# A decoder layer on one core: the side steps of a batch at other tiles of the written order

## The reference, cut to what matters

```
x = x + self_attention(layernorm(x))           # one head of 128, scores 256 x 256 per batch
x = x + cross_attention(layernorm(x), context) # 16 heads of 64, scores 256 x 1601 per head and batch
x = x + chosen_tokens_block(layernorm(x))      # router weight per token; the 31 best of 256 per batch
                                               # go through attention (16 heads of 8) and a GELU layer
```

## Time and profile before

| | |
|---|---|
| median of three executions | 2321.48 us |
| profiled execution | 2324.74 us |
| its span, first to last instruction | 2323.5 us |
| TensorE busy | 2154.8 us, 93% |
| GpSimd busy | 1916.2 us, 82% |
| ScalarE busy | 1844.7 us, 79% |
| VectorE busy | 1799.3 us, 77% |
| mean granted TensorE clock | 0.990 of full speed |
| first tile's exponential | 47.3 us |
| last tile's exponential | 2276.4 us |

### The profile page before, as it was taken

The page is one execution under the profiler, slowest core; times in us unless marked ns, Lnnn a source line. Parts: engine busy times, 40 slices in busy tenths (PEclk is TensorE's granted clock), DMA queues, the critical chain, the costliest instruction groups (busy, mean ns, idle before and its releaser), DMA issues.

```text
span 2323.5 us, 58064 instructions
## 1 busy us (share of the span) xinstructions
PE 2154.8 (93%) x22151; PEld 1566.6 (67%) x22151; DVE 1799.3 (77%) x3728; ACT 1844.7 (79%) x3125; POOL 1916.2 (82%) x1112
## 2 busy tenths in 40 slices
PE   8899999999998999999999899999999999999998
PEld 5567666766766666676767666677676666667665
DVE  5777878787787878877787888877878778786765
ACT  4788887888886888887978778788787788778872
POOL 1789888988987888888888788888898888888992
PEclk8999999999999999999999999999999999999999
DMA  2010000000000000000000000000000000000000
GB/s 67 28 49 13 1 2 12 2 13 1 12 2 1 12 2 13 2 11 12 2 12 2 1 12 2 12 2 21 2 2 12 2 12 2 2 2 11 2 1 10
DMA packets 17221, 22.15 MB, mean 10 GB/s; under 512 B 5601, under 2 KB 14834, under 8 KB 16946
## 3 DMA queue, kind: packets, MB, share of 16 engines
q1 hardware_dynamic: 15842, 18.24, 2.8%
q10 hardware_dynamic: 1104, 0.20, 0.1%
HBM read 16.20 MB, written 2.10 MB: 8 GB/s over the span
## 4 chain that ended last, share of the span: by engine, by line
PE 32%; DVE 7%; ACT 7%; issue 6%; POOL 2%; DVEq 0%; ACTq 0%; POOLq 0%
PE PS L525 6%; PE PS L563 5%; PE PS L526 5%; PE PS L542 5%; PE PS L544 4%; PE PS L589 3%; DVE EH L1026 2%; ACT PF L844 2%; POOL EL L1496 2%; DVE over L1049 2%; ACT over L866 1%; ACT EH L851 1%; PE PS L573 1%; ACT AH L880 1%; PE PS L599 1%
## 5 line engine op out<-in xcount | busy, mean ns | idle before, releaser
L1496 POOL TENSOR_TENSOR EL<-PF,EH 124x1024 f16<-124x1024 f32 x828 | 1761.2, 2149 | 255.1 <-ACT PF L844 75.0
L844 ACT ACTIVATE PF<-PS 124x512 f32<-124x512 f32 x1664 | 978.8, 600 | 264.1 <-PE PS L526 249.6
L542 PE MATMUL PS<-Ch,EH 123*128 123x97 f16 (+1 forms) x6656 | 768.0, 207 | 65.6 <-POOL EL L1496 50.9
L542 PEld LDWEIGHTS PS<-Ch,EH 123*128 123x128 f16 (+1 forms) x6656 | 608.8, 98 | 239.2 <-issue 123.7
L544 PE MATMUL PS<-Cl,EL 123*128 123x97 f16 (+1 forms) x6656 | 764.7, 207 | 0.0
L1026 DVE TENSOR_SCALAR_CACHE_REDUCE EH<-PF 124x1024 f16<-124x1024 f32 x621 | 746.7, 1208 | 20.1 <-ACT PF L844 18.7
L544 PEld LDWEIGHTS PS<-Cl,EL 123*128 123x128 f16 (+1 forms) x6656 | 598.6, 98 | 167.4 <-issue 3.0
L1049 DVE CUSTOM_DVE_ANT_1 over<-over,PS 128x806 f32<-128x806 f32 x512 | 506.4, 989 | 223.8 <-PE PS L563 132.9
L525 PE MATMUL PS<-AH,ChT 97*124 97x512 f16 x1664 | 648.9, 390 | 26.3 <-ACT PF L844 24.8
L526 PE MATMUL PS<-AL,ClT 96*124 96x512 f16 x1664 | 635.5, 382 | 0.0
L866 ACT ACTIVATE over<-PS 128x806 f32<-128x806 f32 x512 | 431.8, 843 | 46.9 <-PE PS L563 23.9
(11 more groups left out here) (234 smaller groups left out, 1834.7 us busy)
## 6 DMA issues: line engine op xcount, KB each, us to landing
Cf<-in_ctx SPq DMA_DIRECT2D x16, 546.0 KB
X<-in_x SPq DMA_DIRECT2D x16, 128.0 KB, 2.3
out_x<-X SPq DMA_DIRECT2D x16, 128.0 KB, 1.7
msk<-in_attention_mask SPq DMA_DIRECT2D x4, 256.0 KB, 4.3
AH<-mh SPq DMA_DIRECT2D x63, 2.0 KB
Cf<-in_ctx SPq DMA_DIRECT2D x16, 53.6 KB
xWqT<-in_xWqT SPq DMA_DIRECT2D x2, 256.0 KB, 6.3
xWo<-in_xWo SPq DMA_DIRECT2D x2, 256.0 KB, 3.8
```

Of the source, the lines that this page charges most:

```text
L542: pe.matmul(PS[:, 6, u0:u0 + DC + 1], EH[0:kr, r, qs], Ch[j][0:kr, t, :], start=(t == 0 and q == 0), stop=False, skip_group_check=True)
L844: act.activation(PF[:, n % PRING, :], PS[0:KP, 4 + n % 2, :], ACT.Exp).then_inc(sg("ex"), 1)
L1496: pool.tensor_tensor(EL[:, r - 1:r + 1, :], PF[:, f - 1:f + 1, :], EH[:, r - 1:r + 1, :], ALU.subtract).then_inc(sg("lo_pool"), 1)
```

## The change

Only places in the written order change. No step is added or removed, and no instruction is another.

- Self attention: first four steps from tiles 4, 6, 8, 10 to 5, 7, 10, 12; `sa_turn` from 30 to 29; its layer norm from 36 to 37.
- Context split: `ctx_hi` from tiles 9 and 11 to 8 and 7 (second half first).
- Choice: `sel_row` from 34 to 35, the first `sel_count` from 35 to 33, the second from 37 to 38, `sel_rank` from 44 to 48.
- Context transposes: the first from 58 to 55, `keys` from 63 to 64.
- Scale: `ctx_max` from 60 to 58, `sigma` from 71 to 68, `ctx_scale` from 75 to 73; `ln0` from 99 to 101.
- Sums' turns: both transposes of a quarter two tiles earlier, `proj` as before. In a batch they stand at 19 and 21, 45 and 47, 71 and 73, 97 and 99.
- Chosen tokens: six places per batch (82, 84, 86, 88, 90, 97) become five (82, 83, 84, 87, 94). The gather stands at 82 of a group's first batch in both. Rotation (`c_rope`): from tile 89 to 95 of the first batch. Values, turned queries and keys (`c_val`, `c_tqk`, `c_keys`): from 90, 97 and 98 of the first batch to 82, 83 and 84 of the second. The last steps (`c_down`, `c_scat`) go from the third batch to the fourth.

```
-SA_PLACES = (4, 6, 8, 10, 30, 32, 56)
-SEL_PLACE = 34
-TURN_PLACES = (58, 60, 62, 64)
-SIGMA_PLACE = 71
-CHOSEN_PLACES = (82, 84, 86, 88, 90, 97)
+SA_PLACES = (5, 7, 10, 12, 29, 32, 56)
+SEL_PLACE = 35
+TURN_PLACES = (55, 60, 62, 64)
+SIGMA_PLACE = 68
+CHOSEN_PLACES = (82, 83, 84, 87, 94)
...
-                 (SEL_PLACE + 1, ("sel_count", b - 1, 0)), (SEL_PLACE + 3, ("sel_count", b - 1, 1)),
-                 (SEL_PLACE + 10, ("sel_rank", b - 1))]
+                 (SEL_PLACE - 2, ("sel_count", b - 1, 0)), (SEL_PLACE + 3, ("sel_count", b - 1, 1)),
+                 (SEL_PLACE + 13, ("sel_rank", b - 1))]
...
-        todo += [(SIGMA_PLACE - 11, ("ctx_max", b + 2)), (SIGMA_PLACE, ("sigma", b + 2)),
-                 (SIGMA_PLACE + 4, ("ctx_scale", b + 2))]
-        todo += [(95, ("ln_stats0", b + 2)), (99, ("ln0", b + 2))]
+        todo += [(SIGMA_PLACE - 10, ("ctx_max", b + 2)), (SIGMA_PLACE, ("sigma", b + 2)),
+                 (SIGMA_PLACE + 5, ("ctx_scale", b + 2))]
+        todo += [(95, ("ln_stats0", b + 2)), (101, ("ln0", b + 2))]
...
-        todo += [(split + 1, ("ctx_hi", n, 0)), (split + 3, ("ctx_hi", n, 1))]
+        todo += [(split, ("ctx_hi", n, 0)), (split - 1, ("ctx_hi", n, 1))]
...
-        todo += list(zip(TURN_PLACES, transposes_of(n))) + [(TURN_PLACES[1] + 3, ("keys", n))]
+        todo += list(zip(TURN_PLACES, transposes_of(n))) + [(TURN_PLACES[1] + 4, ("keys", n))]
...
-        todo += list(zip((*q[:6], q[5] + 4, q[5] + 10, q[6]), self_attention(n)[2:]))
+        todo += list(zip((*q[:6], q[5] + 5, q[5] + 10, q[6]), self_attention(n)[2:]))
...
-        for late, step in ((1, ("turn_u", 0)), (3, ("turn_u", 1)), (5, ("proj",))):
+        for late, step in ((-1, ("turn_u", 0)), (1, ("turn_u", 1)), (5, ("proj",))):
```

## The result

The changed kernel takes 2263.07 us (median of 4 runs, 2257.95 to 2267.62) beside 2322.68 us for the kernel before on the same chip (2320.55 to 2326.45): ratio 0.9741, 95% interval 0.9713 to 0.9769. That is 60 us less where 43 were forecast; 2263.07 lies 15 us under the forecast, inside its range. Between the two profiled executions it is 57.1 us: span 2266.4 against 2323.5. (The profiled execution of the changed kernel is the longest of its four, 2267.62 us.)

What follows compares the result with a forecast made beforehand. TensorE, busy 93% of the span, was taken as the bound, so only its idle time could change. 3.0 us per batch times 14, plus 0.5 each for batches 0 and 15, gave -43: 2278.5 us, range 2262 to 2292.

Steps and rivals of the forecast that it cites:

- Start, 0.9: Self attention and context split, tiles 4 to 14: earlier exponentials on ScalarE win 0.9 us per batch, bounds 0 and 1.21.
- Choice, 1.7: Selection and sums' turns, tiles 26 to 50: 0.63 plus 1.30 us of waits won, taken as 1.7 per batch.
- gone or under 0.3 us: Sign: TensorE's waits at tiles 13, 14, 34, 40, 50 and 77 vanish or fall under 0.3 us each.
- Context turns, sigma, 0.3: Tiles 55 to 77: 0.7 and 0.66 us won, 0.45 and 0.6 lost, sum 0.3 us per batch.
- the rest, 0.1: Layer norm at tile 101 and the turns at 97 and 99: 0.1 us won per batch.
- Chosen tokens, 0: Chosen tokens' steps at their new places: 0 for a group of four batches, bounds -7 and +21 us.
- Some 4 us again: Rotation at tile 95 holds the fold of tile 96, which TensorE needs at 99: a wait of some 4 us.
- Rival 3: Slower: steps at 82, 83, 84 share one bank; 7.35 us per group batch, 66 in all, 2344.5 us; chance 0.13.
- Batch 15, -0.5: Last batch, which has no self attention: 0.5 us won.
- Rival 2: Key products at tile 84 stretched beside a fed GpSimd: 6 us lost per group, 18 in all, 2296.5 us; chance 0.12.
- Rival 1: GpSimd's run is the real bound: only 1.0 us per batch won, 14 in all, 2307 us; chance 0.15.
- Rival 4: Nearly all idle time goes, 4.5 us per batch, and four low clocks (12 us): 2246.5 us; chance 0.07.

Runs made afterwards that it cites:

- the start alone: Kernel before with only self attention's first four steps at tiles 5, 7, 10, 12 and the context split's first halves at 8 and 7: 2298.11 us, ratio 0.9897.
- the spread places: Changed kernel with chosen steps that use the bank two tiles apart or more, on own places in each of a group's four batches: 2237.37 us, ratio 0.9625.
- the chosen places alone: Kernel before with only the chosen tokens' new places (82, 83, 84, 87, 94): 2333.81 us, ratio 1.0046.
- the choice without the rank: Kernel before with row at 35, counts at 33 and 38, self attention's turn at 29, layer norm at 37, rank still at 44: 2315.89 us, ratio 0.9963.
- the context steps alone: Kernel before with context transposes from 55, keys 64, maxima 58, sigma 68, scaling 73, layer norm 101, sums' turns unmoved: 2324.5 us, ratio 1.0005.
- the turns alone: Kernel before with only both transposes of the sums two tiles earlier: 2377.49 us, ratio 1.0221.
- the context steps with the turns: Kernel before with context transposes, keys, maxima, sigma, scaling and layer norm at their changed places, plus the sums' transposes two tiles earlier: 2379.74 us, ratio 1.0236.
- the rank alone: Kernel before with only the rank block moved from tile 44 to 48: 2296.74 us, ratio 0.9892.

## Why the prediction was right, point by point

- **Start, 0.9.** Right in its mechanism, and small: 1.3 alone. I held back 0.3 for a chain on VectorE (low split, maxima) that turned out to leave ScalarE only 0.32 us. TensorE's two waits were 1.21. Batch 0, put at 0.5, won 4.1, and 3.6 of that comes with the start alone.
- **Choice, 1.7.** Right. The parts measured are 0.5 (choice) and 1.5 (rank), 2.0 against the 1.93 summed; GpSimd's run did take back most of the 0.79 and 1.55. The rank brought 0.2 more than its wait. The early count was covered by 1.0 us, the figure of the prediction. The sign "gone or under 0.3 us" failed at tile 40 (0.45), and another 0.67 stands at 42.
- **Context turns, sigma, 0.3, and the rest, 0.1.** Too small: 1.1 together. From tile 52 to 78 they win 0.4, near the 0.3, but by errors against each other: at tile 61 only 0.26 of the 0.7 were won (0.77 to 0.51), at tile 56 0.28 were lost and not 0.45, and of the 0.6 behind sigma there is no wait over 0.1 us from tile 62 to 75 (0.43 at tile 76, where TensorE waited 0.28 before). "The rest, 0.1" is what was too small: 0.2 us by tile 16 and 0.55 from tile 90 on, where waits of 0.40 and 0.22 us at tiles 100 and 102, which the prediction did not list, are gone. "The turns cost nothing" was argued from the age of the sums alone; the bank they need was left out. It holds beside sigma at 68, where they even win time, and fails at 71 (1.72 us).
- These four measured alone make 1.3 + 0.5 + 1.5 + 1.1 = 4.4 of the plain batch's 4.75 us, where I summed 3.0. This is the term that was mis-sized, by 1.75 us or 24.5 in 14 batches. The other 0.35 is, to 0.02, what the turns win right ahead of tile 50 and what is lost again there while the rank is at 44: from tile 49 to 50 the changed kernel's lead over the kernel before grows from 2.01 to 2.34 us, and nothing takes it back. The forecast gave too small a gain here by 24.5 us, in batch 0 by 3.6 and ahead of it by 2.7, and too large a one by 8.0 for the chosen tokens and by 9.2 in batch 15. So it is partly luck that the time came within 15 us of it.
- **Chosen tokens, 0.** The sum came out near (8 us lost over batches 4 to 14), but not by the steps given. "Some 4 us again" behind the rotation at tile 95 failed. Of its products, VectorE's timeline in batch 4 says:

```profile
702.24 0.56 DVE L1347 TENSOR_TENSOR QR<-QK,XS 128x128 f32<-128x128 f32 x1
702.72 0.28 DVE L1348 TENSOR_TENSOR QR<-QK,XS 128x128 f32<-128x128 f32 x1
```

  0.28 us where it was 2.22: at that place GpSimd is at the layer norm and not in a subtraction, and TensorE waits at most 0.15 us from there to the batch's end. Batches 4, 8 and 12 win 12.7 each, of which 4.75 is the plain batch's and 3.4 the low clock's. Against that stand new waits, as in batches 5 and 6 (tiles 90 and 87 of TensorE's timeline):

```profile
832.20 0.43 PE L525 MATMUL PS<-AH,ChT 97*124 97x512 f16 x1 [2.96 <-ACT PF L844]
...
833.38 0.38 PE L525 MATMUL PS<-AH,ChT 97*124 97x512 f16 x1
...
835.27 0.63 PE L525 MATMUL PS<-AH,ChT 97*124 97x512 f16 x1
...
966.93 0.69 PE L797 MATMUL PS<-ident,GTt 128*128 128x128 f32 x2 [2.74 <-DVE hn L1330]
```

  Behind the first wait the same matmul takes 0.38 us and two microseconds later 0.63: the clock has fallen (for 3.4 us in either batch). Next to a plain batch's gain batches 5 and 6 lose 3.2 and 3.7 us, 9 and 10 4.1 and 5.4. Batches 7 and 11, now with the last chosen steps, stand 5.8 us above a plain one, 3.9 of it TensorE's own work on them. Rival 3 had put 7.35 on each. Its mechanism, though, is not what the rows show. A wait for the one bank, a tile behind its last user, looks like this (batch 5, tile 83):

```profile
820.18 0.41 PE L758 MATMUL PS<-ident,QR 128*128 128x128 f32 x2 [0.21 <-DVE VX L1356]
```

  In batch 6, where the step reads its neighbour's data too, it is 0.19 at tile 84. The long waits stand behind chains on VectorE that hold a stretched instruction. VectorE and ScalarE in batch 5, then VectorE in batch 6:

```profile
821.51 4.31 DVE L1363 TENSOR_TENSOR KX<-fqkT,headmask 128x512 f32<-128x512 f32 x4 [1.47 <-ACT fqkT L961]
```

```profile
831.04 0.62 ACT L965 ACTIVATE SC<-SC 128x496 f32<-128x496 f32 x1 [5.23 <-DVE SC L1380]
```

```profile
964.68 2.20 DVE L1330 SCALAR_TENSOR_TENSOR hn<-XA,ss,ln2r 128x128 f32<-128x128 f32 x1 [0.95 <-POOL ss L1437]
```

  In batch 5 ScalarE comes to the exponential of the chosen scores and stands 5.23 us, while VectorE does the key products, its roundings and folds and the scores; the tiles' exponentials queue behind. In batch 6 the normalised rows `hn` take 2.20 us, where their like takes 0.35, and their reader stands one tile behind. With the spread places `hn` still takes 2.21, but the reader comes later and waits 1.21 us for something else; batch 6 is 4.8 us shorter. That points to the distance to the step whose data are read, more than to the distance to the bank's last user; no run moves one of the two alone.
- **Batch 15, -0.5.** Wrong: +8.7. The prediction left out that the last chosen steps (`c_down`, `c_scat`) now stand in this batch, which had none. VectorE and GpSimd around its tile 83, then TensorE:

```profile
2187.43 0.29 DVE L1404 TENSOR_TENSOR XA<-PS,XA 128x128 f32<-128x128 f32 x1 [2.73 <-PE PS L810]
2187.76 4.36 DVE L1406 TENSOR_SCALAR XA<-XA,XS 128x128 f32<-128x128 f32 x1
```

```profile
2185.73 6.30 POOL L1496 TENSOR_TENSOR EL<-PF,EH 124x1024 f16<-124x1024 f32 x3
...
2197.97 2.13 POOL L1496 TENSOR_TENSOR EL<-PF,EH 124x1024 f16<-124x1024 f32 x1 [5.93 <-ACT PF L844]
```

```profile
2192.18 1.22 PE L818 MATMUL PS<-XA,KX 32*128 32x128 f32 x4 [3.99 <-DVE XA L1406]
```

  A multiply of 0.29 us in the kernel before took 4.36 and ended with GpSimd's third subtraction (2185.73 + 6.30 = 2192.03). TensorE waited 3.99 us and then had half the clock for 13.7 us. With the step two tiles later (the spread places) it takes 0.29 again and the batch 120.8. So the stretch, with the low clock behind it, cost up to 8.4 us here and 5.5 in the other trace of this kernel (126.3); the spread places move the neighbouring steps too. The page "SBUF — State Buffer" of the Trainium skill, section "Who interferes with whom", names a multiply by a scalar operand among the instructions that can enter a mode with two ports and then contend with GpSimd, and says that one blocks for the other's whole instruction. The trace agrees with the first. It goes past the second: the multiply began 0.07 us before the first of the three subtractions ended, and both that followed went ahead of its end.
- **Rival 2** (keys stretched beside a fed GpSimd) did not come about for the products it named: in batch 5 the first takes 2.50 us but the others 0.68, and in the kernel before one of the four took 2.62 at tile 99 already. So the change added nothing there. The same mechanism struck in batches 6 (`hn`) and 15, where I had not looked.
- **Rivals 1 and 4.** Rival 1 fell: GpSimd's run took back most of two waits, but the start's 1.3 us went through it whole. Rival 4's term for the plain batch (4.5 us, nearly all idle time) is what came, 4.75; its other half did not: the four low clocks went, but seven others came, and the time lies 17 us above its 2246.5.
- **Clock.** "The low clock in at most four places" failed: it is at half in seven, 41.0 us in all, where it was in four of 6.8 (27.3), head and tail left out. But none of the seven stands near tile 50. The kernel before has one there, in batch 7; the start alone has one, the chosen places alone one, the choice without the rank none and the context steps alone two, all with waits of 1.27 to 1.31 us at tile 50. With 1.62 us the turns alone have two, the context steps with the turns ten. None of the kernels in which the rank has moved shows one there.

What stays open: why the clock falls near tile 51 in some batches and not in their likes, and how long it stays low. The length of the wait alone doesn't decide it, since the same 1.62 us was followed by a fall in ten of 15 batches of one kernel and in two of 15 of another.

## What to carry to other kernels

Where nothing is added or removed, sum the waits of the bounding engine in one plain batch, follow each to the engine that ended it, and move what stands ahead of it there; then look at the odd batches (the first, the last, those with extra steps) one by one, for that is where the same edit costs. A step's tile is two claims, on the engine's order and on the bank it turns over: an edit that loses 12 us alone (the chosen places ending at 94) was worth 19 beside the others, because it freed the tile that another of them (the turn at 97) needs. Before a small VectorE instruction with its operands in SBUF is put somewhere, look whether GpSimd is in a row of long instructions there. And a wait that moves or grows is no loss by itself: see first whether its end has moved.

## What the runs showed of the hardware

- VectorE instructions with their operands in SBUF took far longer beside GpSimd's subtractions of 2.13 us: the multiply above 0.29 to 4.36 us, `hn` 0.35 to 2.20, a key product 0.68 to 2.50, `rank` with two elements 0.16 to 1.19. `rank` ended some 0.02 us behind the end of a subtraction in each of batches 1 to 15, in the traces of the kernel before, the changed one and the rank alone.
- A half clock can cost more than the wait ahead of it, and not always the same: 3.99 us of wait were followed by 13.7 us at 1.2 GHz in one execution and by 6.8 in another of the same kernel.
- A wait of 1.62 us ahead of the projection came before a halved clock in ten of 15 batches of one kernel and in two of 15 of another; one of 1.27 to 1.31 us at the same place in none, one or two of 15.
